# The last gathers of a two-layer MoE + SSM kernel: five row groups accumulate into the result, three keep a buffer that VectorE adds

## The chip, the cores and the metric

One core of one Trainium2 chip. The metric is the device time of one execution of the whole program, in microseconds; smaller is better.

## The reference, cut to what matters

A tensor x of 2 x 2048 tokens of 256 floats goes through an FFN, a state-space mixer, and the same FFN again ("layer one" and "layer two" below are the two FFNs). The part that the change touches is the end of the second FFN:

```
shared_out = _swiglu(x, shared_gate, shared_up, shared_down)
logits = x @ gate_w.T
top_id = argmax(logits); score = sigmoid(max(logits)); xs = x * score[:, None]
for each expert e of 8:                      # every token has exactly one expert
    routed_out += _swiglu(where(top_id == e, xs, 0), wg, wu, wd)
...
x = x + 0.5 * (shared_out + routed_out)      # of the layer-normed x; the last line of all
return x
```

So each output row is the residual row, plus half of a shared expert's row, plus half of one routed expert's row.

## The kernel before, in words

The 4096 tokens are 32 tiles of 128 rows (one row per partition), in 8 groups of 4 tiles. `acc` in SBUF holds the residual of all tokens (128 x 32 x 256 floats) and is in the end stored to `out`, group by group (512 KB each).

Each FFN runs like this on TensorE (PE). The shared expert runs over 5 of the groups; then the routed experts run over 39 sorted slots of 128 rows in a hardware loop (`routed_slots`); then the shared expert runs over the last 3 groups (`shared(L, 1)`). In layer two the order of groups is 6, 7, 0, 1, 2, then the slots, then 3, 4, 5. Every float32 product is three matmuls (`mm3`, L382 to L384). For one group, `shared_gu` makes gate and up in four blocks (fb 0 to 3, 12 matmuls each), ScalarE (ACT) makes silu (L855) and a rounding (L839), VectorE (DVE) multiplies (L1232) and makes the remainder (L1130), `shared_down` is 48 shorter matmuls, and DVE adds half of the result to `acc` in two halves (`add_shared`, L1280). TensorE may start block fb (2 or 3) only after DVE's product of block fb-2.

The routed results are stored slot by slot to `ys_sorted` in HBM. When all are stored (`y_all_stored`), GpSimd (POOL) fetches each token's row back with indirect DMAs, one for each tile of 128 rows, four for a group, by the row numbers in `pos`. In layer one each of these DMAs adds into `acc` in flight (`gather_tile`, L1784, `compute_op=ALU.add`). In layer two they write into a buffer `yr` (L1889), in the order of groups 3, 4, 6, 7, 0, 1, 2, 5, and DVE adds the buffer to `acc` (`add_rows`, L1341, 128 x 1024 floats) at places that `ADDED` fixes: group 3 and 4 while group 3's shared part runs, 6, 7 and 0 during group 4's, 1, 2 and 5 during group 5's. L1717 is the indirect DMA that scatters rows to the sorted order before the slots.

SyncE (SP) issues the stores of `out`: seven at L2003, each after a wait for DVE's add (`s_fad`) and, for 3 and 4, for the shared part (`s_add`), then group 5 in two halves (L2008). The semaphore `s_fin[g]` counts the landed gathers of a group (16 for each DMA).

Of the kernel before, what the change touches and what calls it, by code (L numbers as in the profile page):

```python
# [18 lines left out]
F32 = mybir.dt.float32  # L19
# [3 lines left out]
ALU = mybir.AluOpType  # L23
# [3 lines left out]
P = 128  # L27
# [3 lines left out]
def build(nc, x, w_routed, w_shared, gate_w, w_in, w_out, vecs, b_in, b_out, ssm_a, ssm_bc, ssm_d, out):  # L31
# [4 lines left out]
    T, H = x.shape  # L36
# [4 lines left out]
    FB = W // (2 * KB * P + H)  # L41
    F = FB * P
    CB = C // P
    GT = 4
    GN = GT * P
    NT = T // P
    NG = NT // GT
    NB = 2
    GB = NG // NB
    NH = NG // 2  # L50
# [11 lines left out]
    ot = out.rearrange("(t p) h -> p t h", p=P)  # L62
    xs_dram = nc.dram_tensor("xs_sorted", (NS * P, H), F32, kind="Internal").ap()
    ys_dram = nc.dram_tensor("ys_sorted", (NS * P, H), F32, kind="Internal").ap()
# [7 lines left out]
    with ExitStack() as ctx:  # L72
        def sb(name, shape, dt, stack=ctx):
            return stack.enter_context(nc.sbuf_tensor(name, shape, dt))

        def sem(name):
            return ctx.enter_context(nc.semaphore(name))


        acc = sb("acc", [P, NT, H], F32)  # L80
# [37 lines left out]
        pos = sb("pos", [P, NT], I32)  # L118
# [43 lines left out]
        routed.close()  # L162

        final = ExitStack()
        yr = sb("yr", [P, NT, H], F32, final)
        final.close()

        early = ExitStack()
# [108 lines left out]
        s_add = sem("shared_added")  # L277
# [18 lines left out]
        s_fin = [sem(f"last_gathered{g}") for g in range(NG)]  # L296
        s_fad = sem("gathered_rows_added")
        s_out = sem("out_stored")
# [38 lines left out]
        def tiles(buf, g, n=GT):  # L337
            return buf[:, bass.ds(g * GT, n), :] if not isinstance(g, int) else buf[:, g * GT:g * GT + n, :]
# [7 lines left out]
        ORDER = ((0, 7, 1, 2, 4, 5, 6, 3), (6, 7, 0, 1, 2, 3, 4, 5))  # L346

        def half_groups(L, half): return ORDER[L][1:NH + 1] if half == 0 else ORDER[L][NH + 1:]

        def c_s(L, g): return L * NG + ORDER[L].index(g)  # L350
# [18 lines left out]
        def group_of(n): return n % NB * GB + n // NB  # L369
        def n_of(g): return g % GB * NB + g // GB  # L370

        ADDED = [{2: (3,), 4: (4,)}, {0: (6,), 1: (7,), 3: (0,)}, {0: (1,), 1: (2,), 2: (5,)}]

        def added(g):

            return 1 + [row_group for place in ADDED for fb in sorted(place) for row_group in place[fb]].index(g)

        def live(n): return 0 <= n < NG

# [748 lines left out]
        def _(dve):  # L1128
# [30 lines left out]
            def ln2_stats(n):  # L1159
                wait_apart(dve, s_ga[group_of(n)], 64)  # L1160
                if n >= 2:
                    dve.wait_ge(s_xa, n - 1)
                norm_stats(n, group_of(n), n % 2, s_st2, s_mv2)
# [57 lines left out]
            def slot_experts(src):  # L1221

                chained(dve.tensor_tensor(se[:, :, :], sidx[:, :, :].to_broadcast([1, NS, E - 1]),
                                       src[0:1, 0:E - 1].unsqueeze(1).to_broadcast([1, NS, E - 1]), ALU.is_ge))
                chained(dve.tensor_reduce(sef[:, :], se[:, :, :], AX.X, ALU.add))
                dve.tensor_copy(slot_e[:, :], sef[:, :]).then_inc(s_tab, 1)

            def s_mult(L, g, fb):
                q = 4 * c_s(L, g) + fb
                dve.wait_ge(s_sg, q + 1)  # L1230
                dve.wait_ge(s_u, q + 1)
                dve.tensor_tensor(hf[:, fb % 2, :], sg[:, fb % 2, :], U2[fb % 2][:, :],  # L1232
                                  ALU.mult).then_inc(s_h, 1)

            def s_lo(L, g, fb):
                dve.wait_ge(s_hh, 4 * c_s(L, g) + fb + 1)
                lo(hT_lo[:, fb, :], hf[:, fb % 2, :], hT_hi[:, fb, :]).then_inc(s_hl, 1)
# [22 lines left out]
            def setup_toeplitz_lo():  # L1260
                dve.wait_ge(s_tza, 1)
                lo(tt_lo[:, :], B[1][:, 0:CH], tt_hi[:, :]).then_inc(s_end, 1)
# [20 lines left out]
            def shared_group(L, half, i):  # L1283
                groups = half_groups(L, half)
                g = groups[i]
                n = c_s(L, g)
                for fb in range(FB):
                    if half == 0:
                        for row_group in SCALED[L][i].get(fb, ()):
                            scale_rows(L, row_group)  # L1290
                    if L == 1 and half == 1:
                        for row_group in ADDED[i].get(fb, ()):
                            add_rows(row_group)
                    if fb >= 2:
                        dve.wait_ge(s_hl, 4 * n + fb - 1)
                    if L == 0 and half == 1 and i == 1 and 1 <= fb <= 2:
                        ln2_stats(fb - 1)
                    s_mult(L, g, fb)
                    if L == 0 and half == 1 and i == 0 and fb == 0:
                        w_in_bias()  # L1300
                    if half == 0 and i == 0:
                        if L == 0 and fb == 0:
                            ends[L] = slot_tables(L)
                        if fb == 0:
                            dve.wait_ge(s_sc, L + 1)
                        if fb == 1:
                            slot_experts(ends[L])
                    if L == 0 and half == 0 and fb == 2 and i == 0:
                        setup_response()
                    if L == 0 and half == 0 and fb == 2 and i == 1:  # L1310
                        setup_rows_lo()
                    if L == 0 and half == 0 and fb == 3 and i == 3:
                        setup_toeplitz_lo()
                    if fb > 0:
                        s_lo(L, g, fb - 1)
                s_lo(L, g, FB - 1)
                if g != groups[-1]:
                    xt_lo(c_s(L, groups[i + 1]))
                if L == 0 and half == 0 and i == 2:
                    ls = slice(3 * RG, 4 * RG)  # L1320
                    lo(qq[ls, :], QF[ls, :], qq[ls, :])
                if half == 0:
                    for row_group in SCALED[L][i].get(FB, ()):
                        scale_rows(L, row_group)
                if L == 1 and half == 1:
                    for row_group in ADDED[i].get(FB, ()):
                        add_rows(row_group)
                    dve.wait_ge(s_fad, added(g))
                if half == 0 and g == groups[-1]:
                    m_x_lo(L, 0)  # L1330
                if L == 0 and half == 1 and g == groups[-1]:
                    state_lo(0, 0)
                    state_lo(0, 1)
                    mix_lo(0)
                add_shared(L, g)
# [2 lines left out]

            def add_rows(g):
                dve.wait_ge(s_fin[g], 16 * GT)  # L1340
                dve.tensor_tensor(tiles(acc, g), tiles(acc, g), tiles(yr, g), ALU.add).then_inc(s_fad, 1)  # L1341

            def scale_rows(L, g):

                half = g % 2
                dve.wait_ge(s_rl[half], 16 * (L * NG // 2 + g // 2 + 1))
                for t in range(GT):
                    r = rows[:, half * GT + t, :]
                    ins = dve.tensor_scalar(r, r, score[:, bass.ds(g * GT + t, 1)], None, ALU.mult)
                ins.then_inc(s_scl, 1)  # L1350
# [40 lines left out]
            def w_in_bias():  # L1391

                dve.wait_ge(s_csum, 1)
                for kb in range(KB):
                    ws = wio_raw[:, 0, kb * C:(kb + 1) * C]
                    dve.scalar_tensor_tensor(ws, B[7][:, :], -1.0 / H, ws, ALU.mult, ALU.add).then_inc(s_wfix, 1)
# [214 lines left out]
        def _(pool):  # L1611
# [272 lines left out]
            experts(1)  # L1884
            y_all_stored(1)

            for g in (row_group for place in ADDED for fb in sorted(place) for row_group in place[fb]):
                for tt in range(g * GT, (g + 1) * GT):
                    pool.indirect_dma_start(  # L1889
                        out=yr[:, tt, :], out_offset=None, in_=ys_dram,  # L1890
                        in_offset=bass.IndirectOffsetOnAxis(ap=pos[:, tt:tt + 1], axis=0)).then_inc(s_fin[g], 16)


        @block.sync
        def _(sp):
# [100 lines left out]
            first_loads(1)  # L1996
            routed_slots(1)
            shared_load(1, 5)
            for g in (3, 6, 7, 0, 4, 1, 2):
                sp.wait_ge(s_fad, added(g))  # L2000
                if g in half_groups(1, 1):
                    sp.wait_ge(s_add, 2 * (c_s(1, g) + 1))
                sp.dma_start(tiles(ot, g), tiles(acc, g)).then_inc(s_out, 16)  # L2003
            g = ORDER[1][NG - 1]
            for a in range(2):
                first = g * GT + 2 * a
                sp.wait_ge(s_add, 2 * c_s(1, g) + a + 1)
                sp.dma_start(ot[:, first:first + 2, :], acc[:, first:first + 2, :]).then_inc(s_out, 16)  # L2008
            sp.wait_ge(s_out, 16 * (NG + 1))


# [43 lines left out]
```

## Time and profile before

| | |
|---|---|
| runs | 920.58 us median of 3 (912.49, 920.58, 922.70) |
| profiled execution | 921.99 us, its span 920.2 us, so 1.8 us lie outside the span |
| mean granted TensorE clock | 0.978 |
| busy share of the span | PE 93%, DVE 53%, POOL 49%, ACT 42% |

Read the busy shares as averages over very different stretches; the change is confined to the last 85 us, from the end of the slots (about 833 us) to the end. A row of a timeline gives the start, the duration, the engine, the line and the operation, and in brackets how long the engine was idle before and what ended that. "remote" and "another core or an unknown queue" mean that the profile doesn't show what released the engine.

### The profile page before, as it was taken

What the parts mean: (1) busy time and instruction counts of PE and PEld (TensorE: products, weight loads), DVE (VectorE), ACT (ScalarE), POOL (GpSimd) and SP (SyncE); (2) the same over time, 40 slices, a digit from 0 to 9 for tenths busy, and PEclk for the clock granted to TensorE, in tenths of its full rate; (3) what the DMA queues carried; (4) which work ended last, traced back from release to release, by engine and by line L of the source; (5) the groups of instructions that cost most, each with busy time, mean ns of one, the idle gap of its engine ahead of it and who ended that gap; (6) DMA issues with size and microseconds to landing.
All of it is one profiled execution on the core that took longest, in us unless ns stands there. A gap on an engine that the chain in (4) does not pass through costs nothing.

```text
span 920.2 us, 16294 instructions
## 1 busy us (share of the span) xinstructions
PE 854.0 (93%) x5398; PEld 736.2 (80%) x5399; DVE 487.8 (53%) x1017; ACT 382.2 (42%) x749; POOL 446.8 (49%) x427
## 2 busy tenths in 40 slices
PE   3999989999999999979999999999999999999668
PEld 2788877888888878868888888987888888888357
DVE  6987543333333337588889868664333333334044
ACT  3343223433333334556678674323333333343021
POOL 5627660333333038879999972775113333204710
PEclk9999999999999999999999999999999999999569
DMA  8794562555554133320111126466354645313332
GB/s 298 269 320 156 194 212 103 194 178 199 183 194 166 51 104 53 53 41 12 29 30 34 37 89 233 135 226 239 121 168 150 225 150 181 126 41 92 103 115 92
DMA packets 70781, 128.76 MB, mean 140 GB/s; under 512 B 6746, under 2 KB 61668, under 8 KB 66372
## 3 DMA queue, kind: packets, MB, share of 16 engines
q0 software_dynamic: 15616, 74.33, 25.1%
q1 hardware_dynamic: 54610, 53.63, 18.4%
q8 instruction: 38, 0.62, 0.3%
q14 instruction: 19, 0.16, 0.0%
q10 hardware_dynamic: 498, 0.02, 0.0%
HBM read 91.64 MB, written 36.32 MB: 139 GB/s over the span
## 4 chain that ended last, share of the span: by engine, by line
PE 66%; POOL 9%; DVE 9%; DMA 6%; issue 5%; another core or an unknown queue 3%; ACT 1%; POOLq 0%; ACTq 0%; DVEq 0%; SPq 0%
PE bank L382 19%; PE bank L383 19%; PE bank L384 19%; PE bank L590 4%; POOL xs_sorted L1717 2%; PE bank L559 2%; PE bank L449 2%; POOL v L1689 2%; DMA rows<-xn_kept 2%; DVE v L1421 1%; DMA xs_sorted<-rows,pos 1%; POOL acc L1784 1%; POOL hT_lo L1693 1%; DVE stats L1141 1%
## 5 line engine op out<-in xcount | busy, mean ns | idle before, releaser
L1757 POOL TENSOR_TENSOR wr_lo<-wr_raw,wr_hi 128x3072 fp32r<-128x3072 f32 x14 | 95.1, 6795 | 96.0 <-DMA wr_hi<-w_routed 91.0
L382 PE MATMUL bank<-wr_hi,xT_hi 128*128 x312 | 130.4, 418 | 8.3 <-issue 7.8
L1379 DVE TENSOR_TENSOR hf<-sg,bank 128x512 f32<-128x512 f32 x78 | 53.6, 688 | 134.0 <-PE bank L384 134.0
L383 PE MATMUL bank<-wr_hi,xT_lo 128*128 x312 | 124.0, 397 | 0.0
L384 PE MATMUL bank<-wr_lo,xT_hi 128*128 x312 | 123.1, 395 | 0.0
L1130 DVE TENSOR_TENSOR hT_lo<-bank,hT_hi 128x512 fp32r<-128x512 f32 x78 | 53.9, 691 | 124.4 <-ACT hT_hi L839 124.4
L382 PE MATMUL bank<-xT_hi,ws_hi 128*128 128x512 f32 x256 | 105.0, 410 | 7.8 <-issue 4.1
L384 PE MATMUL bank<-xT_lo,ws_hi 128*128 128x512 f32 x256 | 103.3, 403 | 5.0 <-issue 5.0
L383 PE MATMUL bank<-xT_hi,ws_lo 128*128 128x512 f32 x256 | 103.1, 403 | 3.6 <-issue 3.5
L855 ACT ACTIVATE sg<-bank 128x512 f32<-128x512 f32 x64 | 38.2, 598 | 161.7 <-PE bank L384 109.4
L839 ACT ACTIVATE xT_hi<-bank 128x256 fp32r<-128x256 f32 (+1 forms) x126 | 56.1, 464 | 99.7 <-PE bank L559 89.3
L382 PE MATMUL bank<-wr_hi,hT_hi 128*128 x312 | 93.8, 301 | 1.3 <-DVE hT_lo L1130 1.3
L384 PE MATMUL bank<-wr_lo,hT_hi 128*128 x312 | 87.4, 280 | 0.0
L383 PE MATMUL bank<-wr_hi,hT_lo 128*128 x312 | 87.3, 280 | 0.0
L1717 POOL DMA_INDIRECT xs_sorted<-rows,pos x64 | 64.2, 1004 | 33.2 <-issue 16.5
L918 ACT ACTIVATE sg<-bank 128x512 f32<-128x512 f32 x78 | 46.6, 598 | 78.6 <-PE bank L384 78.6
L1421 DVE SCALAR_TENSOR_TENSOR v<-bank,vec,v 128x511 f32<-128x511 f32 (+2 forms) x96 | 70.9, 746 | 13.5 <-ACT v L988 11.0
L382 PE MATMUL bank<-ws_hi,hT_hi 128*128 128x256 f32 x256 | 74.9, 293 | 2.0 <-issue 1.3
L382 PEld LDWEIGHTS bank<-wr_hi,xT_hi 128*128 128x128 f32 x312 | 58.9, 189 | 21.9 <-issue 10.8
L384 PE MATMUL bank<-ws_lo,hT_hi 128*128 128x256 f32 x256 | 73.4, 287 | 0.6 <-issue 0.6
L383 PE MATMUL bank<-ws_hi,hT_lo 128*128 128x256 f32 x256 | 73.4, 287 | 0.5 <-issue 0.3
L1232 DVE TENSOR_TENSOR hf<-sg,bank 128x512 f32<-128x512 f32 x64 | 43.7, 682 | 52.6 <-PE bank L384 39.8
(234 smaller groups left out, 2132.1 us busy)
## 6 DMA issues: line engine op xcount, KB each, us to landing
wr_raw<-w_routed POOLq DMA_DIRECT2D x16, 1536.0 KB, 7.2
wr_hi<-w_routed POOLq DMA_DIRECT2D x16, 1536.0 KB
rows<-xs_sorted SPq DMA_DIRECT2D x78, 128.0 KB, 2.8
ys_sorted<-rows SPq DMA_DIRECT2D x78, 128.0 KB, 1.8
xn_kept<-xg SPq DMA_DIRECT2D x16, 512.0 KB, 4.6
rows<-xn_kept SPq DMA_DIRECT2D x16, 512.0 KB
xg<-xn_kept SPq DMA_DIRECT2D x12, 512.0 KB
acc<-x SPq DMA_DIRECT2D x8, 512.0 KB, 9.8
```

Source lines behind the costliest of these rows:

```text
L382: pe.matmul(o, a_hi, b_hi, start=start, stop=False, skip_group_check=True)
L383: pe.matmul(o, a_lo, b_hi, start=False, stop=False, skip_group_check=True)
L384: return pe.matmul(o, a_hi, b_lo, start=False, stop=stop, skip_group_check=True)
L839: return act.activation(o, i, ACT.Copy)
L855: act.activation(sg[:, fb % 2, :], G2[fb % 2][:, :], ACT.Silu).then_inc(s_sg, 1)
L918: act.activation(sg[:, 0, :], MG[:, :], ACT.Silu).then_inc(s_msg, 1)
L1130: return dve.tensor_tensor(o, full, f32(h), ALU.subtract)
L1232: dve.tensor_tensor(hf[:, fb % 2, :], sg[:, fb % 2, :], U2[fb % 2][:, :], ALU.mult).then_inc(s_h, 1)
L1379: dve.tensor_tensor(hf[:, 0, :], sg[:, 0, :], MU[:, :], ALU.mult).then_inc(s_mh, 1)
L1421: dve.scalar_tensor_tensor(vb_[:, d:GN], UB[cb % 2][:, 0:GN - d], vec[:, cb, k:k + 1], vb_[:, d:GN], ALU.mult, ALU.add).then_inc(s_tap if ...
L1717: pool.indirect_dma_start(out=xs_dram, out_offset=bass.IndirectOffsetOnAxis(ap=pos[:, tt:tt + 1], axis=0), in_=rows[:, half * GT + t, :], ...
L1757: pool.tensor_tensor(wr_lo[:, e % 2, :], wr_raw[:, :], f32(wr_hi[:, e % 2, :]), ALU.subtract).then_inc(s_wl, 1)
```

## The change

`yr` shrinks from 32 tiles to 12 (groups 3, 4 and 5, called `LATE`). The gathers of groups 6, 7, 0, 1 and 2, whose shared part was added to `acc` long before, use the accumulating form of layer one. The order of the gathers becomes 6, 7, 3, 0, 4, 1, 5, 2. DVE has three `add_rows` left in place of eight: group 3's in block 3 of group 4, group 4's in block 2 of group 5, group 5's at the end of group 5 just before its `add_shared`. The stores of `out` follow the new order: for an accumulating group SP waits for the landed gathers alone; the last store is that of group 2.

```diff
-        yr = sb("yr", [P, NT, H], F32, final)
+        yr = sb("yr", [P, (NT // GT - NH - 1) * GT, H], F32, final)
...
-        ADDED = [{2: (3,), 4: (4,)}, {0: (6,), 1: (7,), 3: (0,)}, {0: (1,), 1: (2,), 2: (5,)}]
...
+        LATE = half_groups(1, 1)
+        ADDED = [{}, {3: (LATE[0],)}, {2: (LATE[1],), FB: (LATE[2],)}]
+
+        GATHERED = (6, 7, LATE[0], 0, LATE[1], 1, LATE[2], 2)
+
+        def added(g): return 1 + LATE.index(g)
...
-                    dve.wait_ge(s_fad, added(g))
+                    if g == LATE[-1]:
+                        dve.wait_ge(s_fad, added(g))
...
             def add_rows(g):
                 dve.wait_ge(s_fin[g], 16 * GT)
-                dve.tensor_tensor(tiles(acc, g), tiles(acc, g), tiles(yr, g), ALU.add).then_inc(s_fad, 1)
+                if g != LATE[-1]:
+                    dve.wait_ge(s_add, 2 * (c_s(1, g) + 1))
+                dve.tensor_tensor(tiles(acc, g), tiles(acc, g), yr[:, bass.ds(LATE.index(g) * GT, GT), :],
+                                  ALU.add).then_inc(s_fad, 1)
...
-            for g in (row_group for place in ADDED for fb in sorted(place) for row_group in place[fb]):
-                for tt in range(g * GT, (g + 1) * GT):
+            pool.wait_ge(s_add, 2 * (NG + NH + 1))
+            for g in GATHERED:
+                if g not in LATE:
+                    gather(g, s_fin[g])
+                    continue
+                for t in range(GT):
                     pool.indirect_dma_start(
-                        out=yr[:, tt, :], out_offset=None, in_=ys_dram,
-                        in_offset=bass.IndirectOffsetOnAxis(ap=pos[:, tt:tt + 1], axis=0)).then_inc(s_fin[g], 16)
+                        out=yr[:, LATE.index(g) * GT + t, :], out_offset=None, in_=ys_dram,
+                        in_offset=bass.IndirectOffsetOnAxis(ap=pos[:, g * GT + t:g * GT + t + 1], axis=0)
+                    ).then_inc(s_fin[g], 16)
...
-            for g in (3, 6, 7, 0, 4, 1, 2):
-                sp.wait_ge(s_fad, added(g))
-                if g in half_groups(1, 1):
-                    sp.wait_ge(s_add, 2 * (c_s(1, g) + 1))
+            for g in GATHERED[:6]:
+                if g in LATE:
+                    sp.wait_ge(s_fad, added(g))
+                else:
+                    sp.wait_ge(s_fin[g], 16 * GT)
                 sp.dma_start(tiles(ot, g), tiles(acc, g)).then_inc(s_out, 16)
-            g = ORDER[1][NG - 1]
+            g = LATE[-1]
             for a in range(2):
                 first = g * GT + 2 * a
                 sp.wait_ge(s_add, 2 * c_s(1, g) + a + 1)
                 sp.dma_start(ot[:, first:first + 2, :], acc[:, first:first + 2, :]).then_inc(s_out, 16)
+            g = GATHERED[-1]
+            sp.wait_ge(s_fin[g], 16 * GT)
+            sp.dma_start(tiles(ot, g), tiles(acc, g)).then_inc(s_out, 16)
```

## Rows read from the trace of the kernel before

**Rows 1.** The page, the span in 40 slices of 23 us: PE and its clock.

```profile
PE   3999989999999999979999999999999999999668
...
PEclk9999999999999999999999999999999999999569
```

**Rows 2.** The chain that ended last, 843 to 885 us: start, duration, what.

```profile
849.35 1.13 DVE acc L1341
850.48 31.38 another core or an unknown queue
```

**Rows 3.** Busy time of each engine by stretch; the last three: clock, DMA share, GB/s.

```profile
837.00:849.00 12.00, 12.00 (x74) 10.66 (x73) 6.83 (x11) 5.18 (x9) 9.26 (x10) 1.00 0.40 121
849.00:882.00 33.00, 18.38 (x43) 10.20 (x41) 1.53 (x3) 0.00 (x0) 21.86 (x23) 0.56 0.33 93
337.00:359.00 22.00, 22.00 (x120) 18.10 (x119) 12.62 (x21) 8.20 (x14) 18.38 (x12) 1.00 0.62 122
```

**Rows 4.** Timeline of PE and of ACT around the stretch 849 to 885 us.

```profile
850.14 0.28 PE L382 MATMUL bank<-ws_hi,hT_hi 128*128 128x256 f32 x1 [0.76 <-issue]
...
881.16 0.59 PE L384 MATMUL bank<-xT_lo,ws_hi 128*128 128x512 f32 x1 [0.81 <-issue]
885.02 0.79 PE L382 MATMUL bank<-xT_hi,ws_hi 128*128 128x512 f32 x1 [3.27 <-DVE hf L1232]
...
882.03 1.08 ACT L855 ACTIVATE sg<-bank 128x512 f32<-128x512 f32 x2 [33.41 <-remote]
```

**Rows 5.** Timeline of POOL: indirect DMAs of layer two, layer one, and scatters.

```profile
836.72 1.03 POOL L1889 DMA_INDIRECT yr<-ys_sorted,pos  x1 [40.34 <-DMA ys_sorted<-rows]
...
849.47 1.84 POOL L1889 DMA_INDIRECT yr<-ys_sorted,pos  x1 [0.30 <-issue]
...
876.62 0.94 POOL L1889 DMA_INDIRECT yr<-ys_sorted,pos  x1 [0.30 <-issue]
...
337.28 1.70 POOL L1784 DMA_INDIRECT acc<-ys_sorted,pos  x1 [0.30 <-issue]
...
358.82 1.54 POOL L1784 DMA_INDIRECT acc<-ys_sorted,pos  x1 [0.30 <-issue]
...
69.39 1.28 POOL L1717 DMA_INDIRECT xs_sorted<-rows,pos  x1 [1.59 <-DVE rows L1349]
...
78.65 0.96 POOL L1717 DMA_INDIRECT xs_sorted<-rows,pos  x1 [0.30 <-issue]
```

**Rows 6.** By source line, both kinds of gather: count, ns min/median/max, first and last start.

```profile
L1889 POOL DMA_INDIRECT yr<-ys_sorted,pos x32: 942/946/1840, 836.7 to 876.6; - x32
...
L1784 POOL DMA_INDIRECT acc<-ys_sorted,pos x32: 1530/1554/2461, 337.3 to 471.7; - x32
```

**Rows 7.** Timeline of DVE: layer one's shared groups, then layer two's.

```profile
347.62 0.69 DVE L1232 TENSOR_TENSOR hf<-sg,bank 128x512 f32<-128x512 f32 x1 [1.44 <-PE bank L384]
...
353.42 1.41 DVE L1280 SCALAR_TENSOR_TENSOR acc<-bank,acc 128x512 f32<-128x512 f32 x2 [2.53 <-PE bank L384]
...
370.96 1.41 DVE L1280 SCALAR_TENSOR_TENSOR acc<-bank,acc 128x512 f32<-128x512 f32 x2 [2.53 <-PE bank L384]
...
843.35 1.22 DVE L1341 TENSOR_TENSOR acc<-acc,yr 128x1024 f32<-128x1024 f32 x1 [2.84 <-DMA yr<-ys_sorted,pos]
...
845.80 0.69 DVE L1232 TENSOR_TENSOR hf<-sg,bank 128x512 f32<-128x512 f32 x1
...
899.31 1.34 DVE L1280 SCALAR_TENSOR_TENSOR acc<-bank,acc 128x512 f32<-128x512 f32 x2 [2.60 <-PE bank L384]
...
916.92 0.69 DVE L1280 SCALAR_TENSOR_TENSOR acc<-bank,acc 128x512 f32<-128x512 f32 x1 [1.40 <-PE bank L384]
```

**Rows 8.** DMA issues of 833 to 921 us and of 336 to 360 us: KB, us from issue to landing.

```profile
out<-acc SPq DMA_DIRECT2D x7, 512.0 KB, 3.0
...
out<-acc SPq DMA_DIRECT2D x2, 256.0 KB, 2.1
...
acc<-ys_sorted,pos POOLq DMA_INDIRECT x12, 3.8
```

More of the change, by code:

```diff
@@ L370, in n_of @@
         def n_of(g): return g % GB * NB + g // GB
-        ADDED = [{2: (3,), 4: (4,)}, {0: (6,), 1: (7,), 3: (0,)}, {0: (1,), 1: (2,), 2: (5,)}]
-        def added(g):
-            return 1 + [row_group for place in ADDED for fb in sorted(place) for row_group in place[fb]].index(g)
+        LATE = half_groups(1, 1)
+        ADDED = [{}, {3: (LATE[0],)}, {2: (LATE[1],), FB: (LATE[2],)}]
+        GATHERED = (6, 7, LATE[0], 0, LATE[1], 1, LATE[2], 2)
+        def added(g): return 1 + LATE.index(g)
         def live(n): return 0 <= n < NG
```

## The prediction

> **What bounds the kernel now.** I read the page first. TensorE is busy nearly everywhere at full clock, except in the last three of 40 slices: there its busy digits are 6, 6, 8 and those of the clock 5, 6, 9 [rows 1]. These three slices are the stretch that the change touches, so all that follows is about the last 85 us.
>
> The chain of work that ended last, cut to that stretch, holds one huge piece: after DVE's second `add_rows`, which ends at 850.48, 31.4 us go to "another core or an unknown queue" [rows 2]. This is a one-core kernel, so it is a wait that the profile cannot explain. The busy times by stretch say what it looks like: from 849 to 882 us PE did 43 matmuls in 33 us at a mean clock of 0.56, where it had done 74 in the 12 us before; ACT did nothing; DVE only the add it had begun and one after the hole; POOL went on with 23 gathers [rows 3]. The timeline of PE shows matmuls one by one with issue gaps before them, with nothing named that they wait for; ACT's silu of group 4, whose input was among the first of those matmuls, starts only at 882.03, after 33.4 us of idleness, in the same instant as DVE and just after PE's last slow matmul ended (881.16 + 0.59 = 881.75) [rows 4]. So PE creeps, and what it signals reaches DVE and ACT late. I call this the stall.
>
> What it costs: without it, `add_shared` of group 3 would follow its last multiply (845.80) after the 5.8 us of layer one (347.62 to 353.42), at 851.6. DVE did it after the stall at about 882. That is some 30 us out of 920, by far the largest thing in the tail.
>
> What goes on beside it is POOL's run of 32 plain gathers: first start 836.72, last 876.62, end 877.56 [rows 5]. The stall begins 12.5 us after this run does, at its eleventh gather (itself lengthened to 1.84 us) and ends 4 us after the run. Two comparisons decide what I think of it. In layer one POOL issues 12 accumulating gathers back to back from 337.28 to 360.36 [rows 5], beside the same shared-expert work, and PE is busy 22.00 of 22 us at clock 1.00 [rows 3]. And the plain indirect DMAs of the scatter, of the same pace as layer two's gathers, come at most 8 in a row (69.39 to 79.61) [rows 5], and PE's busy share shows no hole there [rows 1]. The only run of more than 8 plain ones is the one with the stall.
>
> **The change part by part.**
>
> The pace of the gathers. A plain one takes 946 ns, an accumulating one 1554 [rows 6], with 0.30 us between. Counted with their irregularities, the plain pace is (876.62 - 836.72) / 31 = 1.29 us, the accumulating one (358.82 - 337.28) / 11 = 1.96 us [rows 5]. After the change 20 are accumulating and 12 plain, the latter in fours. POOL's run grows from 41 us to 20 x 1.96 + 12 x 1.29 = 54.7 us; by the medians it is 20 x 1.85 + 12 x 1.25 = 52.0. Started at 836.72, it ends between 888.7 and 891.4. Its new wait for `s_add` is for five groups added before the slots and costs nothing; nothing is queued behind these gathers on POOL.
>
> The stall. I cannot name its mechanism from the trace, so its price is bounded: between gone (minus 30 us) and lengthened with POOL's longer run (plus 13 us). I take gone. The nearest rows are layer one's: same instruction, same neighbours, 12 in a row against 8 at most here. The plain ones now stand in fours, where eight went by without harm.
>
> One rule of the Trainium skill (VectorE: DVE Perf Modes, "The TRN2 errata") warns that dense completion increments of semaphores can lock up another engine, and asks to space them. Each gather increments by 16; its increments would be a third less dense in the accumulating form. The stall looks like a mild case of it, but no row shows the increments themselves. By this rule the sum would be A's below.
>
> DVE's adds. Eight of 1.22 us become three [rows 7]. The first now has DVE wait 2.84 us for its gathers, in the middle of group 3; that goes. The two in front of group 4's blocks (2.4 us) hold back the multiply for which PE waits 3.27 us at 885.02 [rows 4]; that goes too. The remaining adds wait: group 3's gathers are the 12th, landed by 836.7 + 8 x 1.96 + 4 x 1.29 + about 1.3 = 859, wanted at about 863 (block 3 of group 4); group 4's by 872, wanted at about 877. Group 5's are the 28th: issued by 883.5, landed by 885, added by 886. Behind that wait only group 5's own `add_shared` is queued, and PE has then nothing left that waits for DVE. It is due at about 886, so this costs 0 to 1 us.
>
> PE's end without the stall: `add_shared` of group 3 at 851.6; one group takes 370.96 - 353.42 = 17.5 us in layer one, and 916.92 - 899.31 = 17.6 for the last here [rows 7]. So the last `add_shared` starts at 851.6 + 17.5 + 17.6 = 886.7, ends 887.4, and its half store (2.1 us [rows 8]) lands at about 890.
>
> The stores. Before they are bunched after the stall; now SP sends them as gathers land, 512 KB in 3.0 us each [rows 8], six of them before 880. They share the DMA engines with the gathers, whose share is 0.33 to 0.40 of them [rows 3]; since POOL's own pace, not the engines, sets the gathers, I cost this at nothing, with up to 1 us on the last landing. SP's waits come in the order of the gathers, so none holds a ready store back for long; group 5's halves (887) come before group 2's.
>
> The end is therefore POOL's: the last gather starts about 889.4 (1.96 before the end of its slot at 891.4), lands 3.8 us later at 893.2, group 2's store is issued then and lands 3.0 to 3.5 later: a span of 896.5. By the medians it is 894. With the 1.8 us outside the span, 896 to 898; the profiled execution stands 1.4 us above the median of the runs, so I say 897 us.
>
> **The rivals.**
>
> A: forecast, stall gone, POOL's run is the new bound: 897. For: the comparisons above. Against: they are two, and the cause is only inferred.
>
> B: the stall comes late. If it needs ten plain gathers in all, however spaced, it begins in group 5's four at about 880, runs to the end of the gathers at 891, and the last of group 5 (6 to 7 us at full speed, some at half clock) follows: 900 to 907.
>
> C, the other side: the stall belongs to POOL's run beside PE in this tail whatever the form of the gathers (the rows of layer one being lucky in some other way), begins after about 12 us and lasts until the run ends. It then gets longer: the end of the run moves from 877.6 to 891.4, 13 us, less the 2.4 us of adds on PE's path: 920.2 + 13.8 - 2.4 = 931.6, time 933 (by the medians 930). It decides from the point where the stall still begins before group 4's blocks are through. For it: the stall did end 4 us after the last gather. Against: 22 us at full speed in layer one [rows 3].
>
> D: the stall has nothing to do with the gathers: PE's creeping ends when PE itself has no more work ready (881.75, waiting for a multiply), and begins and ends as before. Then the change gives only the 2.4 us: 918. The Trainium skill (SBUF — State Buffer, "Who interferes with whom") says that PE and ACT never wait on anyone for SBUF, and a DMA never contends with a compute engine. By this rule taken widely D would be right. The trace shows a PE that waits for something unnamed during a run of DMAs, so the rule does not cover what is seen here.
>
> **How the numbers follow.** A has 0.58, B 0.12, C 0.17, D 0.13. The likeliest is A: 897. For this kernel about 1% (9.2 us, so 911.4 and 929.8) is what a measurement can tell from no change. Faster by over 1% is A and B, 0.70; within 1% is D, 0.13; slower is C, 0.17. The range runs from 889 (PE's own end at 890, if POOL's run is shorter than I reckon) to 921 (D with its margin) and leaves out C and little else.
>
> **What would show it.** If A is right: PE busy without holes and at clock 1.00 from 833 to about 886; no "unknown queue" of tens of microseconds in the chain; 20 gathers near 1.55 us and 12 near 0.95, ending at about 890; three DVE adds; a chain that ends with POOL, a gather's landing and a store of 512 KB. If B or C: PE's issue gaps and ACT's "remote" wait again, later or longer. If D: the same stall at the same place, with POOL's run going on behind its end. The prediction is wrong by its main term if PE still creeps anywhere beside the gathers; it is wrong in a small term if the accumulating gathers run at another pace beside the stores of `out` than they did in layer one.

## The result, and the profile after

The changed kernel takes 897.35 us, median of 4 runs (894.77 to 898.38), against 920.42 us for the kernel before in the same measurement (4 runs, 912.49 to 922.70): a ratio of 0.9744 (95% interval 0.9706 to 0.9782). 897 was forecast. The 31 us stall of [rows 2] is gone. But the kernel before does not always take 912 to 923 us: beside most of the experiments it took 887 to 899 us, in every one of 83 runs. The one profile of it there has no stall, and there the changed kernel is the slower one, by 0.75%. Both halves belong to the result.

The stretches of the changed kernel that answer to [rows 3]; the columns are those of that group (stretch, its length, busy time of PE, PE's weight loads, DVE, ACT, POOL, then clock, DMA share, GB/s).

```profile
837.00:849.00 12.00, 12.00 (x81) 10.99 (x81) 5.86 (x9) 3.74 (x8) 10.17 (x7) 1.00 0.62 111
849.00:882.00 33.00, 32.69 (x193) 28.78 (x191) 15.40 (x22) 9.79 (x18) 26.60 (x22) 1.00 0.68 164
882.00:896.00 14.00, 0.00 (x0) 0.00 (x0) 2.51 (x3) 0.00 (x0) 4.87 (x3) 0.57 0.49 112
```

Between 849 and 882 us PE now does 193 matmuls at clock 1.00, where it did 43 at 0.56. In the last 14 us it has nothing to do: the end belongs to POOL and the stores. The timelines of POOL, DVE and SP (the last with the span over which its issues lie) say the same; they answer to [rows 5] and [rows 7].

```profile
832.83 1.68 POOL L1789 DMA_INDIRECT acc<-ys_sorted,pos  x1 [40.88 <-DMA ys_sorted<-rows]
...
848.25 0.99 POOL L1898 DMA_INDIRECT yr<-ys_sorted,pos  x1 [0.30 <-issue]
...
878.30 0.95 POOL L1898 DMA_INDIRECT yr<-ys_sorted,pos  x1 [0.30 <-issue]
...
885.95 1.53 POOL L1789 DMA_INDIRECT acc<-ys_sorted,pos  x1 [0.30 <-issue]
...
864.09 1.41 DVE L1281 SCALAR_TENSOR_TENSOR acc<-bank,acc 128x512 f32<-128x512 f32 x2 [2.48 <-issue]
...
883.01 1.22 DVE L1345 TENSOR_TENSOR acc<-acc,yr 128x1024 f32<-128x1024 f32 x1 [5.12 <-DMA yr<-ys_sorted,pos]
884.27 1.29 DVE L1281 SCALAR_TENSOR_TENSOR acc<-bank,acc 128x512 f32<-128x512 f32 x2
...
884.99 0.97 SPq L2019 DMA_DIRECT2D out<-acc  x2
890.13 0.37 SPq L2022 DMA_DIRECT2D out<-acc  x1
```

POOL's run lasts from 832.83 to 887.48, 54.65 us; group 5's add and `add_shared` are through at 885.6; then group 2's gathers land and its store goes out at 890.13.

By line, both kinds of gather, answering to [rows 6] (the 52 are 32 of layer one and 20 of layer two):

```profile
L1789 POOL DMA_INDIRECT acc<-ys_sorted,pos x52: 1532/1558/2471, 334.4 to 886.0; - x52
...
L1898 POOL DMA_INDIRECT yr<-ys_sorted,pos x12: 942/953/993, 848.2 to 878.3; - x12
```

### The profile page after: what moved, and what is told of

Its sections match the earlier page's. It is cut to its first block, busy times and chain, and to the rows that moved or that the text cites. A ratio compares the mean times of both kernels' runs of the same rounds, so it can differ in the third digit from the quotient of the medians.

```text
span 896.0 us, 16288 instructions
## 1 busy us (share of the span) xinstructions
PE 838.5 (94%) x5398; PEld 729.5 (81%) x5399; DVE 482.5 (54%) x1012; ACT 381.9 (43%) x749; POOL 461.4 (51%) x427
## 4 chain that ended last, share of the span: by engine, by line
PE 65%; POOL 14%; DVE 8%; issue 6%; DMA 5%; ACT 1%; POOLq 0%; ACTq 0%; SPq 0%; DVEq 0%
PE bank L383 19%; PE bank L384 18%; PE bank L385 18%; POOL acc L1789 5%; PE bank L591 4%; POOL xs_sorted L1722 2%; PE bank L560 2%; PE bank L450 2%; POOL v L1694 2%; DVE v L1426 1%; DMA rows<-xn_kept 1%; DMA xs_sorted<-rows,pos 1%; POOL yr L1898 1%; POOL hT_lo L1698 1%; DVE stats L1142 1%
## 5 line engine op out<-in xcount | busy, mean ns | idle before, releaser
L1789 POOL DMA_INDIRECT acc<-ys_sorted,pos x52 | 87.3, 1680 | 55.3 <-DMA ys_sorted<-rows 40.9
L383 PE MATMUL bank<-xT_hi,ws_hi 128*128 128x512 f32 x256 | 101.9, 398 | 0.4 <-DVE ws_lo L1548 0.4
L384 PE MATMUL bank<-xT_hi,ws_lo 128*128 128x512 f32 x256 | 100.3, 392 | 0.0
L385 PE MATMUL bank<-xT_lo,ws_hi 128*128 128x512 f32 x256 | 100.1, 391 | 0.0
```

Of the source, the lines that this page charges most:

```text
L383: pe.matmul(o, a_hi, b_hi, start=start, stop=False, skip_group_check=True)
L384: pe.matmul(o, a_lo, b_hi, start=False, stop=False, skip_group_check=True)
L385: return pe.matmul(o, a_hi, b_lo, start=False, stop=stop, skip_group_check=True)
L1789: pool.indirect_dma_start(out=acc[:, tt, :], out_offset=None, in_=ys_dram, in_offset=bass.IndirectOffsetOnAxis(ap=pos[:, tt:tt + 1], axis= ...
```

## The experiments

The theories: P, my reading, the quick succession of plain gathers (their pace, 1.25 us, over more than eight) makes the stall; F, the plain form or the early adds do; D, the stall has nothing to do with the gathers. The kernel before ran beside each experiment. It took either 912 to 923 us or 887 to 899; nothing lay between. Its profile has the stall at 921.99 us and has none at 897.38 (x_before). For its other runs I infer the stall from the time; no trace shows it. A run that tells about the stall needs the first kind beside it.

### Beside a kernel before that stalled

These three are single runs, each with a run of the kernel before next to it.

**e9_paced_again.** The kernel before, with a short operation of POOL behind each gather:

```diff
+    PACE = 512
...
+            paused = 0
...
                     pool.indirect_dma_start(
                         out=yr[:, tt, :], out_offset=None, in_=ys_dram,
                         in_offset=bass.IndirectOffsetOnAxis(ap=pos[:, tt:tt + 1], axis=0)).then_inc(s_fin[g], 16)
+                    paused += 1
+                    pool.memset(idle[:, 0:PACE], 0.0).then_inc(s_idle, 1)
+                    pool.wait_ge(s_idle, paused)
```

> The paced kernel again (32 plain gathers, a memset of 0.5 us behind each, so that they come at 1.85 us), for the case that the kernel before stalls beside it (920 us). Then: if the pace makes the stall, none here, 905 to 912 us as before; if the plain form does, PE creeps from some 12 us after the first gather to 4 us after the last one, and the time is 935 us or more. If the kernel before stands at 888 to 899 beside it, this tells nothing new and is 905 to 912 again.

Measured: 907.28 us, beside 922.84 for the kernel before (one run each). The two stretches of its profile:

```profile
837.00:849.00 12.00, 11.38 (x77) 10.32 (x77) 7.52 (x11) 3.43 (x6) 10.00 (x13) 1.00 0.24 71
849.00:882.00 33.00, 25.48 (x126) 20.94 (x125) 13.53 (x18) 6.91 (x13) 27.59 (x36) 0.90 0.55 165
```

126 matmuls in place of 43. The largest gap of PE from 849 us on has a name, none of its gaps there is put to "issue", and no wait of tens of microseconds is left:

```profile
856.47 0.80 PE L385 MATMUL bank<-xT_hi,ws_hi 128*128 128x512 f32 x1 [4.25 <-DVE hf L1235]
```

It waits for DVE's multiply, which is queued behind an add whose gathers come late at this pace. So 32 plain gathers with the early adds in place made no stall once they were spaced (every (889.42 - 831.42) / 31 = 1.87 us). F falls: neither the form nor the early adds are enough. P stands, by one pair of runs here.

**e8_half_rows.** Every gather and every add with 64 of the 128 rows, so half of the routed part is left out:

```diff
-                dve.tensor_tensor(tiles(acc, g), tiles(acc, g), tiles(yr, g), ALU.add).then_inc(s_fad, 1)
+                dve.tensor_tensor(acc[0:64, g * GT:(g + 1) * GT, :], acc[0:64, g * GT:(g + 1) * GT, :],
+                                  yr[0:64, g * GT:(g + 1) * GT, :], ALU.add).then_inc(s_fad, 1)
...
-                        out=yr[:, tt, :], out_offset=None, in_=ys_dram,
-                        in_offset=bass.IndirectOffsetOnAxis(ap=pos[:, tt:tt + 1], axis=0)).then_inc(s_fin[g], 16)
+                        out=yr[0:64, tt, :], out_offset=None, in_=ys_dram,
+                        in_offset=bass.IndirectOffsetOnAxis(ap=pos[0:64, tt:tt + 1], axis=0)).then_inc(s_fin[g], 16)
```

> The kernel before with every one of its 32 gathers (and DVE's adds) cut to 64 of the 128 rows, so that half of the routed part is left out; each gather still increments by 16, so the increments come about one and a half to two times as densely. If dense increments or a fast run of plain gathers can bring the stall on by themselves, PE creeps here too (over 905 us, issue gaps in the tail). If the stall needs something of the place where the program runs, PE runs through, the gathers are never waited for, and the end is PE's: 886 to 892 us.

Measured: 918.76 us, beside 920.28. The stall is there with half the rows. The gathers came only slightly faster, every (870.16 - 831.80) / 31 = 1.24 us for 1.29, so the expected density was not reached (the increments came some 4% more densely, not one and a half times). And since the kernel before stalled beside it, it does not say what a dense run does elsewhere. But it shows the stall's end better than the first profile. Timelines of POOL and PE:

```profile
831.80 0.97 POOL L1890 DMA_INDIRECT yr<-ys_sorted,pos  x1 [40.92 <-DMA ys_sorted<-rows]
...
870.16 0.90 POOL L1890 DMA_INDIRECT yr<-ys_sorted,pos  x1 [0.30 <-issue]
...
843.88 0.28 PE L383 MATMUL bank<-ws_hi,hT_lo 128*128 128x256 f32 x1 [0.37 <-issue]
...
846.03 0.31 PE L382 MATMUL bank<-ws_hi,hT_hi 128*128 128x256 f32 x1 [1.15 <-issue]
...
870.59 0.37 PE L382 MATMUL bank<-ws_hi,hT_hi 128*128 128x256 f32 x1 [2.43 <-issue]
873.38 0.37 PE L383 MATMUL bank<-ws_hi,hT_lo 128*128 128x256 f32 x1 [2.43 <-issue]
874.79 0.37 PE L384 MATMUL bank<-ws_lo,hT_hi 128*128 128x256 f32 x1 [1.03 <-issue]
875.49 0.58 PE L382 MATMUL bank<-ws_hi,hT_hi 128*128 128x256 f32 x1 [0.33 <-issue]
```

And four stretches by busy time: 844 to 848, 872 to 876, 876 to 880 and 880 to 884 us.

```profile
844.00:848.00 4.00, 1.12 (x4) 0.79 (x4) 0.69 (x1) 0.60 (x1) 2.95 (x4) 0.77 0.19 51
...
872.00:876.00 4.00, 1.25 (x3) 0.85 (x3) 0.00 (x0) 0.00 (x0) 0.00 (x0) 0.50 0.01 4
876.00:880.00 4.00, 3.76 (x11) 2.97 (x11) 2.51 (x3) 0.00 (x0) 0.00 (x0) 0.50 0.03 12
880.00:884.00 4.00, 4.00 (x18) 3.30 (x17) 1.82 (x2) 1.28 (x3) 0.00 (x0) 0.97 0.76 250
```

PE creeps from 843.9, 12 us after the first gather, at the tenth one; in the first profile it was 836.72 and about 849.4, after the tenth one. POOL's last gather ends at 871.06; the gap before a matmul is still 2.43 us at 873.38, then falls to 1.03 and 0.33, and PE is at work without gaps soon after 875.5, in the middle of group 3's `shared_down`, with no work having run out. In the first profile PE happened to have just finished all it could do when the stall ended, which is why D could be held. Here D falls: the end follows POOL's last gather by some 4 us (875.49 - 871.06 = 4.4; 4.2 in the first profile).

The first profile also shows that PE's signals come late, and not only its work. DVE's `add_shared` of group 3 needs the 48 matmuls of `shared_down`; the last of them ended at 855.96, and DVE, idle and with nothing else to wait for, began at 881.95.

**e10_eight_again.** The changed kernel with other groups in each form: 6 and 7 accumulate, the rest is plain, at most eight plain gathers in a row.

```diff
-        ADDED = [{}, {3: (LATE[0],)}, {2: (LATE[1],), FB: (LATE[2],)}]
...
-        GATHERED = (6, 7, LATE[0], 0, LATE[1], 1, LATE[2], 2)
...
+        ADDED = [{}, {1: (3,), 2: (0,), 3: (1,)}, {0: (4,), 3: (2,), FB: (5,)}]
...
+        GATHERED = (3, 0, 6, 1, 4, 7, 2, 5)
...
-                if g not in LATE:
+                if g in (6, 7):
                     gather(g, s_fin[g])
```

> The version with 24 plain and 8 accumulating gathers, at most eight plain ones in a row, again, for the case that the kernel before stalls beside it (over 915 us). Then: if breaking the fast run after eight gathers is enough, it has no stall and takes 887 to 897 us, less than the changed kernel. If what counts is the mean pace over a longer time (here 1.46 us, between the 1.25 of the stalling and the 1.71 of the changed kernel), the stall comes, perhaps late: 900 to 920 us. If the kernel before stands at 888 to 899 beside it, it tells nothing new.

Measured: 896.33 us, beside 921.13. Its profile between 849 and 882 us has 166 matmuls at 0.95. One issue gap of PE, 0.44 us at 851.87, is all that looks like creeping. One wait has no name: DVE stands 4.42 us before group 1's add, which begins at 867.03, and PE then waits 1.86 us for what DVE makes next. The last of group 1's gathers started at 860.08 and landed 4.41 us later, so some 2.5 us of that wait stay unexplained. 24 plain gathers made no stall where four slower ones stood between one eight and the next.

```profile
849.00:882.00 33.00, 30.70 (x166) 26.92 (x166) 15.82 (x21) 8.28 (x15) 26.91 (x21) 0.95 0.69 175
```

Together with the first measurement, all nine runs of this kind with a quick succession of 32 gathers were slow (912 to 923 us: the kernel before eight times, with its profiled run, and e8_half_rows). None of the six without it was: the changed kernel four times at 895 to 898, 907.28 and 896.33.

### Beside a kernel before that did not stall

**e1_paced**, the same kernel as e9_paced_again:

> The kernel before, with a POOL memset of 128 x 512 floats (some 0.5 us) behind every one of the 32 plain gathers, so that they come at about 1.85 us instead of 1.25, the pace of accumulating ones; nothing else changed. If the stall comes from the pace of the gathers (theory P, my reading), there is no stall: PE runs at full speed through the tail, POOL's run takes about 60 us, and the end is that run's: about 903 to 908 us in all. If it comes from the plain form, or from the place of DVE's adds (theory F), the stall stands beside the longer run: 930 us or more. If the stall has nothing to do with the gathers (theory D), about 920.

Measured: 910.53 us (2 runs) against 894.28 (21 runs): the 903 to 908 forecast for P, a little over, but with no stall to remove it decided nothing then. It does give the price of the spacing where there is no stall: 16 us.

**e2_half_run.** Only 16 gathers; the routed part of the other four groups is left out, and DVE adds group 3's buffer in its place:

```diff
+                src = g if g in (3, 4, 6, 7) else 3
+                dve.tensor_tensor(tiles(acc, g), tiles(acc, g), tiles(yr, src), ALU.add).then_inc(s_fad, 1)
...
-            for g in (row_group for place in ADDED for fb in sorted(place) for row_group in place[fb]):
+            for g in (3, 4, 6, 7):
```

> The kernel before, with only the first 16 gathers (groups 3, 4, 6, 7); the other four groups get group 3's buffer added instead, so their routed part is left out, and DVE's work stays the same. POOL's run then ends at about 857 us instead of 877.6. If the stall is tied to POOL's run, it ends some 4 us after it, at about 861, 20 us earlier: about 900 us in all. If PE's creeping ends only when PE has no work ready (theory D), it still ends at about 882 and the time stays near 920.

Measured: 894.42 us, ratio 0.9989 (0.9949 to 1.0030). Inconclusive, as the kernel before had no stall; e8_half_rows answered its question.

**e3_plain_first.** The changed kernel's 12 plain gathers first, then its 20 accumulating ones:

```diff
-            for g in GATHERED:
+            for g in LATE + tuple(g for g in GATHERED if g not in LATE):
```

> The changed kernel with its 12 plain gathers (groups 3, 4, 5) in a row at the start and the 20 accumulating ones behind them; the same DMAs, adds and stores otherwise. If a run of more than about 10 plain gathers starts the stall, it starts at about 848 us; then either it ends soon once the slower accumulating ones follow (a few us lost, 898 to 905), or it holds until POOL's run ends at about 890 (925 to 932). If the form alone decides, that is if the plain ones do no harm in any number below 32, the time is that of the changed kernel, 897.

Measured: 899.12 us (8 runs), ratio to the kernel before 1.0063 (1.0021 to 1.0105). Its profile has no stall, and neither had the kernel before, so it is inconclusive for the stall.

**e4_all_plain.** The late places and nearly the order of the change, all gathers plain:

```diff
-        ADDED = [{}, {3: (LATE[0],)}, {2: (LATE[1],), FB: (LATE[2],)}]
...
-        GATHERED = (6, 7, LATE[0], 0, LATE[1], 1, LATE[2], 2)
...
+        ADDED = [{}, {1: (6,), 2: (7,), 3: (LATE[0],)}, {0: (0,), 1: (1,), 2: (LATE[1],), 3: (2,), FB: (LATE[2],)}]
...
+        GATHERED = (6, 7, LATE[0], 0, LATE[1], 1, 2, LATE[2])
...
-                if g not in LATE:
-                    gather(g, s_fin[g])
-                    continue
```

> The changed kernel's order of groups and its late places for DVE's adds, but all 32 gathers plain into a full buffer, back to back, and DVE adds all eight groups (group 5's last). If the long fast run makes the stall, it is there again from about the eleventh gather on, and the time is 915 to 925 us. If the early adds of group 3 and 4, or SyncE waiting without issuing stores, made it, it is gone: POOL's run of 41 us ends before PE, and the end is PE's, about 888 to 892 us.

Measured: 888.99 us (8 runs), ratio 0.9972 (0.9930 to 1.0014). The time is that of the second case, but since the kernel before had no stall beside it, this is no evidence that the early adds made it. Nor is its end PE's alone, as the expectation had it:

```profile
885.11 1.23 DVE L1346 TENSOR_TENSOR acc<-acc,yr 128x1024 f32<-128x1024 f32 x1 [2.05 <-DMA yr<-ys_sorted,pos]
```

The last gather starts at 880.67, later than a pace of 1.29 us would have it (42.67 / 31 = 1.38 us), and DVE stands 2.05 us for it before the last add.

**x_before and x_after**, both kernels unchanged:

> The kernel before, unchanged, once more with a profile. The shared runs of it in the first set of experiments stood at 894.28 us (21 runs, 888 to 899), not at 920. If the stall is a thing of the place where a program runs, this profile has either none (about 894 us, PE without issue gaps in the tail) or the full one (about 920), and never something between.

> The changed kernel, unchanged, beside the kernel before in the same rounds. Where the kernel before has no stall, my sum for the two ends still holds: POOL's run of 54.7 us, a landing and a 512 KB store set the end of the changed one, PE's end that of the one before, so the changed one should be slower by 1 to 6 us, about 897 against 894. If instead the change gains by something other than the stall, it stays faster here too.

Measured: 889.13 us for the kernel before (10 runs, 887 to 897; shared runs beside it 891.97), 900.84 for the changed one, ratio to the kernel before 1.0075 (1.0039 to 1.0111). The profile of the undisturbed kernel before, the stretches of [rows 3]:

```profile
837.00:849.00 12.00, 12.00 (x65) 10.28 (x64) 5.36 (x8) 4.31 (x8) 7.80 (x8) 1.00 0.46 132
849.00:882.00 33.00, 30.46 (x172) 26.46 (x171) 19.97 (x27) 8.86 (x16) 24.62 (x24) 0.95 0.65 196
```

And two of its waits (who waited for whom: us in total, times, longest):

```profile
DVE acc L1341 <- DMA yr<-ys_sorted,pos: 14.6, 5, 3.8
...
PE bank L382 <- DVE hf L1232: 2.5, 1, 2.5
```

The same 32 plain gathers, from 838.93 at nearly the same pace (40.70 / 31 = 1.31 us), and PE does 172 matmuls where it did 43. By e9_paced_again and e10_eight_again the quick succession is needed for the stall; by this profile it is not enough. The eleventh gather is lengthened here too (1.56 us at 851.70), so that is no sign of the stall.

Two rivals can be set aside from the traces. One is timing: perhaps PE and POOL meet at another point of their work. Group 4's transposes start 7.67 us after the first gather with the stall (844.39 - 836.72) and 7.68 without it (846.61 - 838.93):

```profile
844.39 1.04 PE L449 MATMUL bank<-ident,xg 128*128 128x128 f32 x8
```
```profile
846.61 1.04 PE L449 MATMUL bank<-ident,xg 128*128 128x128 f32 x8
```

The other is that PE's program arrives late. In x_before the DMA queue q8, marked "instruction", moves one packet about every 24 us, and I take it for PE's. In the first profile it moves one at 838 us and the next at 892. From 885.02 until then PE works without a gap, so it had its instructions at hand all along.

**e5_runs_of_eight**, the kernel of e10_eight_again:

> A third version: only groups 6 and 7 accumulate, the other six are plain, in the order 3, 0, (6), 1, 4, (7), 2, 5, so that at most eight plain gathers follow one another; DVE's six adds lie late, where their gathers have landed. POOL's run is 8 x 1.96 + 24 x 1.29 = 46.6 us; its last gather lands some 48 us after the first starts, which is a little before PE needs it. If PE's end sets the time, as in the all-plain run with late adds (889 us), this gives 888 to 891, some 8 to 10 us less than the changed kernel and 0 to 5 less than the kernel before where that has no stall. Where the kernel before stalls (920 us) and runs of up to eight plain gathers are harmless, it is still 888 to 891; if it stalls as well, 905 to 920.

Measured: 893.79 us against 895.24, ratio 0.9988 (0.9955 to 1.0022): the same as the kernel before. The forecast 888 to 891 was some 3 us too low, and 0 to 5 us less than the kernel before can't be told from nothing here.

**e6_form_alone.** The accumulating form with the old order and places of the adds:

```diff
-        ADDED = [{}, {3: (LATE[0],)}, {2: (LATE[1],), FB: (LATE[2],)}]
...
-        GATHERED = (6, 7, LATE[0], 0, LATE[1], 1, LATE[2], 2)
+        ADDED = [{2: (3,), 4: (4,)}, {}, {2: (5,)}]
...
+        GATHERED = (3, 4, 6, 7, 0, 1, 2, 5)
```

> The change's form alone: the gathers of groups 6, 7, 0, 1 and 2 accumulate, but the order 3, 4, 6, 7, 0, 1, 2, 5 and the places of the adds for 3, 4 and 5 are those of the kernel before. Counted from the first gather, POOL's run takes 54.7 us, group 5's add (in block 2 of group 5) then waits until about 56, and PE's last 7 to 8 us and a 256 KB store of 2.7 us follow: 67 us in place of the 56.7 of the undisturbed kernel before. Where that one takes 889 to 897 us this gives 900 to 907. Where the kernel before stalls (920 us), the form should keep the stall away and the same 900 to 907 should stand; if the stall stands beside this form too, over 925.

Measured: 907.30 us (4 runs) against 895.96, ratio 1.0126 (1.0079 to 1.0172), at the upper edge of the 900 to 907 forecast. DVE stands up to 15.8 us for gathers, and PE up to 13.5 us for what DVE makes behind them.

**e7_last_swapped.** The last two groups of gathers in the other order:

```diff
-        GATHERED = (6, 7, LATE[0], 0, LATE[1], 1, LATE[2], 2)
+        GATHERED = (6, 7, LATE[0], 0, LATE[1], 1, 2, LATE[2])
```

> The changed kernel with the last two groups of gathers swapped: group 2 (accumulating) before group 5 (plain). POOL's run is as long, 54.7 us, but behind it stand a plain landing (1.3 us), DVE's add (1.2) and add_shared (1.3) and a store of 256 KB (2.7) in place of an accumulating landing (2.7) and a store of 512 KB that took 5.9 us to the end of the span. If the tail of the changed kernel is POOL's run plus what follows its last gather, this ends 2 us earlier, at 61 us from the first gather instead of 63.2: about 898 to 899 where the changed one has 901. If PE sets the end, it stays the same as the changed one.

Measured: 898.31 us against 894.68, ratio 1.0051 (1.0014 to 1.0088). In its profile the first gather starts at 829.71 and the span ends at 892.0, 62.3 us for the 61 forecast and the 63.1 of x_after. The interval overlaps that of x_after, so the 2 us forecast for the swap are not shown.

The start of the tail differs from profile to profile (829.7 to 838.9 us), although the programs are the same up to there. So the tails compare best from the first gather to the end of the span:

| kernel | first gather | end of span | between |
|---|---|---|---|
| before, with the stall | 836.72 | 920.2 | 83.5 |
| x_before | 838.93 | 895.6 | 56.7 |
| after | 832.83 | 896.0 | 63.2 |
| x_after | 836.68 | 899.8 | 63.1 |
| e4_all_plain | 838.00 | 890.5 | 52.5 |
| e5_runs_of_eight | 834.22 | 890.5 | 56.3 |
| e10_eight_again | 837.71 | 894.5 | 56.8 |
| e6_form_alone | 837.19 | 905.4 | 68.2 |

The tail of the changed kernel is 63 us long, beside a stalling kernel before or not; that of the kernel before is 84 or 57. One profile each, so a microsecond between two rows means little.

## Why the prediction was right, point by point

The stall, its price and its removal. "Gone, minus 30 us" held where the kernel before has the stall: 83.5 - 56.7 = 27 us is what it costs. That it is tied to POOL's run is shown by its end in e8_half_rows. That spacing the gathers keeps it away is shown by e9_paced_again, where only a short operation and a wait for it were added (one run, but with the kernel before at 922.84 next to it), and nine slow runs out of nine against none out of six bear it out. The form as such is not shown to matter: accumulating gathers come every 1.85 us in place of 1.25, and by e9_paced_again that alone would do. The comparison with layer one, on which the prediction leaned, could not tell form from pace. What the prediction did not see is that the stall depends on something outside the kernel. It treated one profile and three runs as the kernel's time; 83 later runs are as short as the one profiled without a stall. That the measurement met the kernel before at 920 us is luck: beside one of 887 to 899 us the same 897 would have been no gain.

What decides whether it comes is open. It isn't the chip: on one and the same chip the kernel before took 888 to 898 us in seven runs and 922.84 at another time. All the times with the stall come from the first measurement and from the experiments timed by a single run, all those without it from experiments timed in repeated rounds; the traces show nothing of what differs. The mechanism within the chip is open too; whether taking the profile has a part in it is not tested either.

POOL's run: forecast 54.7 us by the paces of layer one, measured 54.65. That this would be the new bound is right: PE is idle for the last 14 us.

PE's end. Group 5's `add_shared` was forecast 50.0 us after the first gather and began at 884.27 - 832.83 = 51.4. DVE stood 5.1 us waiting for group 5's gathers; they landed 4.7 us after the last one started, where I had taken about 2.6 (a slot of 1.29 and 1.3 behind it), as at the quiet start of the old run. Other gathers and stores were in flight beside them; that they caused the delay is not shown. It cost the end nothing.

The end. The last gather took 4.2 us to land (forecast 3.8). The last store was forecast at 3.0 to 3.5 us and took 5.9 to the end of the span. Its packets moved between 891 and 893 us:

```profile
891.00:892.00 1.00, 0.00 (x0) 0.00 (x0) 0.00 (x0) 0.00 (x0) 0.00 (x0) 0.50 0.95 327
892.00:893.00 1.00, 0.00 (x0) 0.00 (x0) 0.00 (x0) 0.00 (x0) 0.00 (x0) 0.50 0.59 198
893.00:894.00 1.00, 0.00 (x0) 0.00 (x0) 0.00 (x0) 0.00 (x0) 0.00 (x0) 0.50 0.00 0
```

and three microseconds follow in which the profile shows nothing. So this term was 2.6 us too small, the landing 0.4, and the last gather's start, 53.1 us after the first, 0.4 late; the tail started 3.9 us earlier than in the profile that I summed on. These happened to cancel: 897 forecast, 897.35 measured. The hit to the microsecond is luck; the sum is good to about 3 us.

DVE's adds and their places. Three adds, none in front of a multiply that PE waits for: right, the profile lists no gap of PE in the tail before its work ends. The old cost was misread, though. Only one add (at 883.16) stands in front of the multiply for which PE waits 3.27 us; the next (884.89) stands behind it. So at most 1.2 of the 2.4 us lay there; the term is in the sums of C and D, not in the one that gives 897. Without the stall the profiles hint that the places are worth more: late places alone go with a tail of 52.5 us in place of 56.7 (e4_all_plain), but its ratio, 0.9972 (0.9930 to 1.0014), doesn't show it. The accumulating form in the old places makes the tail 68.2 (e6_form_alone). With late places the form costs 63.1 - 52.5 = 10.6 us of tail, and 899.12 - 888.99 = 10.1 us between e3_plain_first and e4_all_plain, because it makes POOL's run the bound.

The rivals. A came about. B (ten plain gathers in all) is contradicted by e10_eight_again, which has 24. C, the slower side by way of a longer stall, did not come; but a slower changed kernel did, elsewhere, by a mechanism that I had only as part of A: POOL's longer run against an undisturbed kernel before. I should have priced it as a rival. D is refuted by e8_half_rows (one profile) and by the missing stall of e9_paced_again. The rule of the Trainium skill (SBUF — State Buffer, "Who interferes with whom") by which PE waits on no one for SBUF gives no account of this stall. The Trainium skill's warning about dense semaphore increments (VectorE: DVE Perf Modes, "The TRN2 errata") agrees with the sign of e9_paced_again, spacing removes the stall, and no run here isolates the increments from the gathers themselves.

No version beats both kernels everywhere by a margin that can be seen. The one with eight accumulating gathers stood at 896.33 us where the kernel before took 921.13 (one run each), and at 893.79 against 895.24 where that had no stall. So it keeps what the change gains, and no cost like the 0.75% can be seen. e4_all_plain has the shortest undisturbed tail and has a quick succession of 32 plain gathers, and was not run beside a kernel before that stalled.

## What to carry to other kernels

An idle time that the profile ascribes to nobody, on three engines at once, may not be part of the kernel's normal time: measure again under other conditions before you credit a change with removing it, and give the gain for both cases. When indirect DMAs run back to back beside full engines, and the profile shows such a hole, space them or break the run, but count POOL's time for them: spacing all 32 cost 16 us here where there was no stall, breaking the run with eight slower ones nothing that can be seen. A slower form in place of an engine's add can become the bound. Place an add on an in-order engine where its data has landed, never in front of an operation that TensorE waits for.

## What the runs showed of the hardware

A run of indirect gathers at 1.24 to 1.29 us each can, after about 12 us, slow TensorE's issue (in e8_half_rows matmuls start 0.7 to 2.8 us apart, the longest after 849.6 us) and leave VectorE idle for 31 us and ScalarE for 33, until about 4 us after the last gather. With 64 rows in place of 128 in each the stall stays. It does not always come: at 1.31 us each x_before has none. At 1.87 us each e9_paced_again had none, beside a kernel before that took 922.84. A gather of 64 rows takes POOL 0.90 us, one of 128 rows 0.95, an accumulating one of 128 rows 1.54 to 1.56: for the plain form the price is nearly all fixed. In e8_half_rows the granted clock averaged 0.77 over the stretch from 844 to 848 us, in which PE's busy time fell to 1.12 of 4 us, was 0.50 through the creeping, which is the lower level of 1.2 GHz, and 0.97 in the stretch from 880 us, after PE had been busy for 3.76 of 4 us.
